# A two-layer graph convolution on one core: batches of twelve tiles instead of eight, rings of two batches, and TensorE's wait for target one-hots placed behind the next gathers

## The reference, cut to what matters

```python
# emb 18750 x 64, W1 64 x 128, W2 128 x 64, edge_index 2 x 300000, r_input 512 x 200
def gcn_conv(x, W, b, src, dst, n):
    h = x @ W
    deg = jnp.zeros((n,), h.dtype).at[dst].add(1.0) + 1.0
    dinv = jax.lax.rsqrt(deg)
    norm = dinv[src] * dinv[dst]
    agg = jax.ops.segment_sum(h[src] * norm[:, None], dst, num_segments=n)
    return agg + h * (dinv * dinv)[:, None] + b
h = gcn_conv(emb, W1, b1, src, dst, 18750)
nodes = gcn_conv(h, W2, b2, src, dst, 18750)
return nodes[r_input.reshape(-1)].reshape(512, 200, 64)
```

## Time and profile before

| what | value |
|---|---|
| median of 3 runs | 2710.62 us (2710.17 to 2713.58) |
| the profiled execution's own time | 2695.12 us |
| its span, first to last instruction | 2693.2 us |
| mean granted TensorE clock in it | 0.867 |
| TensorE matmul busy | 2067.8 us (77%) |
| VectorE busy | 2301.0 us (85%) |
| ScalarE busy | 1928.6 us (72%) |
| GpSimd busy | 927.8 us (34%) |

### The profile page before, as it was taken

One profiled execution on the slowest core, in us unless ns is written; L12 is line 12 of the kernel. 1 busy time (PEld: TensorE's weight loads), 2 busy tenths in 40 slices (PEclk: granted clock), 3 DMA queues, 4 the chain that ended last, 5 costly groups with the idle time before them and its releaser, 6 DMA issues.

```text
span 2693.2 us, 87729 instructions
## 1 busy us (share of the span) xinstructions
PE 2067.8 (77%) x36895; PEld 1728.1 (64%) x36895; DVE 2301.0 (85%) x3709; ACT 1928.6 (72%) x5267; POOL 927.8 (34%) x704
## 2 busy tenths in 40 slices
PE   3455555554562699998889899989999999999980
PEld 2345454444321477787777777867888888888870
DVE  9999999999988689889889999967777777777760
ACT  7868999999663886666666667766777777777760
POOL 2000000000000345426735456314233446666666
PEclk8566666665786899999999999999999999999995
DMA  4000000000021334343347555566776764555531
GB/s 115 0 1 1 1 1 1 1 1 1 18 71 43 107 117 133 118 136 105 98 113 139 123 133 148 147 186 186 211 214 212 210 193 142 139 143 139 145 106 18
DMA packets 191626, 277.10 MB, mean 103 GB/s; under 512 B 122459, under 2 KB 130539, under 8 KB 190973
## 3 DMA queue, kind: packets, MB, share of 16 engines
q1 hardware_dynamic: 168924, 244.05, 28.8%
q0 software_dynamic: 22304, 27.40, 8.3%
HBM read 219.68 MB, written 51.81 MB: 101 GB/s over the span
## 4 chain that ended last, share of the span: by engine, by line
PE 49%; DVE 36%; ACT 6%; issue 4%; POOL 2%; DMA 2%; SPq 0%; DVEq 0%; POOLq 0%
PE ps L1366 27%; PE ps L1315 16%; DVE keys L1610 7%; DVE keys L1611 7%; DVE oh L1946 4%; DVE oh L1460 4%; DVE arena L1460 3%; ACT arena L1118 1%; ACT grow_t L1044 1%; DVE keys L1872 1%; PE ps L1251 1%; DVE keys L1630 1%; DVE keys L1631 1%; PE ps L1341 1%; POOL out L912 1%
## 5 line engine op out<-in xcount | busy, mean ns | idle before, releaser
L1133 ACT ACTIVATE grow_t<-ps 128x384 bf16<-128x384 f32 x2744 | 1144.1, 498 | 525.1 <-PE ps L1315 489.3
L1366 PE MATMUL ps<-grow_t,oh 128*128 128x192 bf16 x10952 | 1054.0, 248 | 4.1 <-issue 3.5
L1366 PEld LDWEIGHTS ps<-grow_t,oh 128*128 128x128 bf16 x10952 | 880.5, 98 | 124.2 <-issue 105.6
L1946 DVE TENSOR_TENSOR oh<-iorep,dl 128x2048 bf16<-128x2048 bf16 x686 | 833.1, 1218 | 118.2 <-PE ps L1366 96.9
L1315 PE MATMUL ps<-arena,keys 128*32 128x192 bf16 x21952 | 608.0, 249 | 63.8 <-DVE keys L1872 23.9
L951 POOL DMA_INDIRECT zring<-table,sidx x296 | 397.2, 1342 | 513.4 <-PE ps L1315 462.7
L1315 PEld LDWEIGHTS ps<-arena,keys 128*32 128x32 bf16 x21952 | 429.2, 97 | 195.1 <-issue 130.4
L859 POOL DMA_INDIRECT arena<-line,row_i x22 | 30.1, 1368 | 832.8 <-DVEq L1688 825.9
L1044 ACT ACTIVATE grow_t<-colf,arena 128x128 bf16<-128x128 f32 x992 | 294.3, 394 | 7.6 <-PE ps L1179 7.6
L1872 DVE TENSOR_SCALAR keys<-keys,rowf 128x2048 bf16<-128x2048 int16 x344 | 260.1, 756 | 30.8 <-DMA keys<-srel 20.8
L1610 DVE TENSOR_TENSOR keys<-keys 128x1280 f32<-128x1280 f32 (+4 forms) x212 | 246.3, 1162 | 13.1 <-ACT keys L1097 9.9
(11 more groups left out here) (246 smaller groups left out, 1912.5 us busy)
## 6 DMA issues: line engine op xcount, KB each, us to landing
keys<-srel SPq DMA_DIRECT2D x344, 512.0 KB
out<-res SPq DMA_DIRECT2D x50, 512.0 KB
table<-arena SPq DMA_DIRECT2D x19, 384.0 KB, 2.8
table<-sgn_l SPq DMA_DIRECT2D x73, 96.0 KB
arena<-table SPq DMA_DIRECT2D x5, 960.0 KB, 8.7
zring<-table,sidx POOLq DMA_INDIRECT x296
nodes<-arena SPq DMA_DIRECT2D x73, 64.0 KB
arena<-in_L_rec_edge_index SPq DMA_DIRECT2D x2, 1171.5 KB, 5.3
```

The lines of the kernel that those rows point to most:

```text
L1133: act.activation(grow[:, (layer * NB + j) % DEEP, h * 2 * ROW:(h + 1) * 2 * ROW], psum[HALF_BANK[layer][HB * j + h][0]][:, 0:2 * ROW], ACT ...
L1366: mm = pe.matmul(sums(sl, k), dwin[:, (layer * NB + j) % DEEP, t // TT, k * P:(k + 1) * P, t % TT], grow[:, (layer * NB + j) % DEEP, t * R ...
L1946: dve.tensor_tensor(dwin[:, (layer * NB + j) % DEEP, 0:made[1], :, :], iorep[:, :, :].unsqueeze(1).to_broadcast(made), dl_h[:, j * BT:j * ...
```

## The change

`BT` goes from 8 to 12, so that a layer has 229 batches of 6 halves (2748 tiles gathered, 10 of them empty, against 2744). `DEEP` goes from 3 to 2: both rings hold 24 tiles as before. Source one-hots are built 12 tiles at a time instead of 16, one build a batch and two batches ahead; their input ring has three places instead of two (`RBUFS`). `AHEAD` is 6 halves, again one batch. TensorE's wait for `d_ready` and `surplus(j)` move behind the gathers of batch j+1. The batch numbers of everything else are scaled by about two thirds: a preparation every 3.5 batches instead of 5, with `TO_QUARTER`, `TO_REL`, `TO_DST` of 3, 6, 8 instead of 4, 9, 12; `LATE_STEP` 2 instead of 3; a guest holds its bank for 3 batches instead of 4. By these numbers there are 42 minis instead of 40.

```diff
-BT = 8
+BT = 12
-DEEP = 3
+DEEP = 2
-RBUFS = 2
-PT = 2 * BT
-NP = -(-NB // 2)
-AHEAD = 4
-LEAD = 7
+RBUFS = 3
+PT = BT
+NP = NB
+AHEAD = HB
+LEAD = 5
...
-        RANKED = 2 * (GT - EARLY) + 1
+        RANKED = -(-2 * 2 * (GT - EARLY) // 3) + 1
...
-            return 5 * (g - 1)
-
-        TO_QUARTER, TO_REL, TO_DST = 4, 9, 12
+            return 7 * (g - 1) // 2
+
+        TO_QUARTER, TO_REL, TO_DST = 3, 6, 8
...
-        ROUNDS, LIST_STEP, LATE_STEP = OU // 8, 5, 3
-        ROUND_AT = LIST_AT + 9
+        ROUNDS, LIST_STEP, LATE_STEP = OU // 8, 3, 2
+        ROUND_AT = LIST_AT + 6
...
-        STORED_AT = [UNITS[1][upto - 1][2] + 10 for upto in UPTO]
-        FILL_FROM, FILL_STEP, FILLS = 20, 3, RT // FILL
+        STORED_AT = [UNITS[1][upto - 1][2] + 8 for upto in UPTO]
+        FILL_FROM, FILL_STEP, FILLS = 17, 2, RT // FILL
...
-                    guest_at[guest] = take(j, guest, j + 4)
+                    guest_at[guest] = take(j, guest, j + 3)
...
-                    wait_ge(rel_out, 16 * (p * PT // P + 1))
+                    wait_ge(rel_out, 16 * (min(p * PT + PT - 1, DO - 1) // P + 1))
...
-                    if x and x % (2 * HB) == 0:
-                        pe.wait_ge(s_ready, layer * NP + FREE + x // (2 * HB) + 1)
+                    if x and x % HB == 0:
+                        pe.wait_ge(s_ready, layer * NP + FREE + x // HB + 1)
...
-                    pe.wait_ge(d_ready, layer * NB + j + 1)
                     if layer == 0:
...
-                    surplus(j)
                     for x in range(HB * j + AHEAD, HB * j + AHEAD + HB):
                         if x < HB * NB:
                             gather_half(x)
 
+                    pe.wait_ge(d_ready, layer * NB + j + 1)
+                    surplus(j)
                     for h in range(HB):
...
                 s_build(0)
+                s_build(1)
...
-                    if j % 2 == 0 and j // 2 + 1 < NP:
-                        s_build(j // 2 + 1)
+                    if j + 2 < NP:
+                        s_build(j + 2)
```

More of the change, by code:

```diff
@@ L513, in gcn_program @@
         LIST_AT = PREPARED + 3
[L514 to L515 removed]
+        ROUNDS, LIST_STEP, LATE_STEP = OU // 8, 3, 2
+        ROUND_AT = LIST_AT + 6
         MASK_AT = ROUND_AT + LIST_STEP * (ROUNDS - 1) + 10
         OVER_AT = MASK_AT + 1
[L518 to L519 removed]
+        LISTED = OVER_AT + 10
+        EARLY_ROUNDS, ROUND_STEP = 6, 4
         PICK_AT = LIST_AT + 5
@@ L522, in gcn_program @@
         DEALS = list(range(0, DONE8, WRAP))
-        ORDER_AT = DEAL_AT + 20
+        ORDER_AT = DEAL_AT + 14
         BAD_AT = ORDER_AT + 2 * (QG + 2)
@@ L526, in gcn_program @@
         LATE = [sl for sl in range(SPE) if close_batch(sl) - 2 < LISTED]
-        FETCHES = [(max(prep_at(g) - 4, 0), "rank", g, 0) for g in range(2, GT)]
+        FETCHES = [(max(prep_at(g) - 3, 0), "rank", g, 0) for g in range(2, GT)]
         FETCHES += [(max(prep_at(g) - 1, 0), "cell", g, 0) for g in range(1, GT)]
-        FETCHES += [(prep_at(g) + 2, "quarter", g, q) for g in range(1, GT) for q in range(1, WIN)]
+        FETCHES += [(prep_at(g) + 1, "quarter", g, q) for g in range(1, GT) for q in range(1, WIN)]
         FETCHES += [(ROUND_AT + LIST_STEP * (u // 8) - 1, "unit", u, 0) for u in range(OU)]
@@ L568, in gcn_program @@
         NU = len(UNITS[0])
-        LAG = 9
+        LAG = 7
         assert all(b[2] - a[2] > LAG + 1 or b[2] == NB for a, b in zip(UNITS[0], UNITS[0][UR:]))
@@ L615, in issued @@
                     if t + 1 in BOUNDS:
-                        scatters += [(max(HB * SCATTER_AT, at + 10 * HB), n) for n in COLS_OF[SET_OF[t]]]
+                        scatters += [(max(HB * SCATTER_AT, at + 7 * HB), n) for n in COLS_OF[SET_OF[t]]]
                 elif scatters and at >= scatters[0][0]:
@@ L798, in _ @@
                     if layer == 0:
-                        for name, g in prep_steps(p - 6):
+                        for name, g in prep_steps(p - 4):
                             if name == "rel":
                                 rel_store(g)
-                        if p == LIST_AT + 1:
+                        if p == LIST_AT + 2:
                             list_rows()
-                        if p == LIST_AT + 5:
+                        if p == LIST_AT + 4:
                             list_load()
-                        if p == DEAL_AT + 7:
+                        if p == DEAL_AT + 6:
                             deal_store()
-                        if p - DEAL_AT - 10 in range(0, 3 * len(DEALS), 3):
-                            deal_load(DEALS[(p - DEAL_AT - 10) // 3])
-                    for unit in units_at(layer, p - 7 - lag):
+                        if p - DEAL_AT - 8 in range(0, 2 * len(DEALS), 2):
+                            deal_load(DEALS[(p - DEAL_AT - 8) // 2])
+                    for unit in units_at(layer, p - 5 - lag):
                         unit_out(layer, *unit)
-                    if p % 2 == 0 and (layer == 0 or p // 2 >= RBUFS):
-                        sources_in(layer, p // 2)
+                    if layer == 0 or p >= RBUFS:
+                        sources_in(layer, p)
                     if layer and p >= FILL_FROM and (p - FILL_FROM) % FILL_STEP == 0 and (p - FILL_FROM) // FILL_STEP <= FILLS:
                         fill_part((p - FILL_FROM) // FILL_STEP)
-                for j in range(NB - 7, NB + lag + 1):
+                for j in range(NB - 5, NB + lag + 1):
                     if layer == 0:
@@ L1141, in _ @@
                     if layer == 0 and 1 <= j < RANKED:
-                        rank(EARLY + (j - 1) // 2, (j - 1) % 2)
+                        for n in range((j - 1) * 3 // 2, min(j * 3 // 2, 2 * (GT - EARLY))):
+                            rank(EARLY + n // 2, n % 2)
                     if layer == 0:
@@ L1828, in prepare @@
                     rows_by_act(EARLY, GT, 2 * (GT - 1))
-                if j == LIST_AT - 5:
+                if j == LIST_AT - 3:
                     dve.sem_inc(over_ready, 1)
@@ L1863, in prepare @@
                     dve.sem_inc(flag_ready, 1)
-            assert PICK_AT > LIST_AT + 2 and FLAG_AT + 20 < NB
+            assert PICK_AT > LIST_AT + 2 and FLAG_AT + 14 < NB
             dve.wait_ge(w_made, 3)
@@ L1870, in s_build @@
                     if p >= SBUFS:
-                        dve.wait_ge(gmm, HB * layer * NB + 2 * HB * (p - SBUFS + 1))
+                        dve.wait_ge(gmm, HB * layer * NB + HB * (p - SBUFS + 1))
                     dve.tensor_scalar(s_oh[:, p % SBUFS, :], srow[:, p % RBUFS, :], rowf[:, 0:1], None, ALU.is_equal).then_inc(s_ready, 1)
```

4 lines of the change are left out of this document (2 added, 2 removed).

## The result

The changed kernel takes 2751.5 us in the median (2749.7 to 2758.9, 4 runs) beside 2712.0 us for the kernel before on the same chip (2710.2 to 2713.6, 4 runs): a ratio of 1.0156 with an interval of 1.0137 to 1.0176. The forecast was 2679 us, its range ended at 2717, and the sign is wrong. Executions that took far longer than the others of their kernel (3202 us in r3, 4224 us in e14) are left out of medians and ratios. Later runs fell on other chips, and there the picture splits. On two more chips the change gave 1.0175 (1.0158 to 1.0192) and 1.0167 (1.0134 to 1.0199); on a fourth it gave 1.0001 (0.9990 to 1.0011), 2679.5 against 2680.5 us. I call the first three chips the first kind (the kernel before takes 2696 to 2712 us there) and the others the second (2680 to 2683 us).

A forecast was written before the change was run, and what follows sets the result against it. TensorE was taken to bound layer 1 and VectorE most of layer 0. Layer 1 -36, layer 0 0 and the end +4.5 summed to -32 us: 2679 us from a median of 2710.6, range 2652 to 2717.

The forecast's parts named there:

- the price of a batch: Layer 1, TensorE: two mode switches of 0.16 us cost 0.32 per batch; 114 fewer batches save 36.5 us.
- the ring of two at nothing: Target one-hot builds: slack shrinks from 2.05 to 1.3 us but stays positive, so two batches of room cost nothing.
- 2655: Rival, layer 0 gains too: the moved wait removes VectorE's 22 us of waits for TensorE; chance 0.16.
- 2715: Rival: the drain is no switch price and grows with the group, so nothing is saved; chance 0.06.
- With no guest in layer 1 ... nothing: Layer 1 PSUM banks: half x takes the bank of half x-6, copied a batch ago, at no cost.
- Bank waits "most hidden": Layer 0: guests' banks make gathers wait 55 us, mostly hidden behind VectorE, busy 99% in 1440 to 1740; +8 us taken.
- banks eat it: Rival, 2708 us: over half of the 55 us of bank waits lie bare, +30 in layer 0; chance 0.12.
- My slack of 1.3 us: Layer 1: a target build has 4.2 us available; the worst batch has 2.9 us in front of d_ready.
- The rival's mechanism: Rival, ring of two, 2742 us: VectorE over 3.3 us a batch makes layer 1 scatters wait for one-hots; chance 0.14.
- The list wait: Layer 0: the 11.6 us wait for GpSimd's surplus list shrinks by 5, to 5 to 7 us.
- the durations of both builds: VectorE: a target build of 3072 columns takes 1.75 us, a source build of 1536 takes 0.62.
- the end: GpSimd alone behind the last gathers: 22 instead of 18 early DMAs are left over, 54 in all, +4.5 us.

The follow-up runs named there:

- r3: The changed kernel with the d_ready wait and surplus products ahead of the next gathers again, first kind of chip: 2770.0 us, 1.0233 of the kernel before.
- e14: Batches of ten tiles with rings of three, guests keeping their bank for 4 batches, second kind: 2664.0 us, 0.9930 of the kernel before.
- e2: The kernel before (eight tiles, rings of three) with only the wait and surplus products moved behind the next gathers, second kind: 2681.5 us, 0.9999.
- e4: The kernel before with GpSimd's 92 early output lookups and stores moved behind the last batch, second kind: layer 1 at 792.8 us.
- e3: The changed kernel with GpSimd's 92 early output lookups and stores moved behind the last batch, second kind: layer 1 at 770.4 us.
- e15: The changed kernel with the 92 lookups and stores behind the last batch, run again, second kind: layer 1 at 781.8 us.
- e16: The changed kernel with the 92 lookups and stores behind the last batch, run once more, second kind: layer 1 at 774.8 us.
- e10: The changed kernel with GpSimd's layer 1 indirect transfers set to start when a gather run has ended, first kind: 2768.4 us, 1.0230 of the kernel before.
- e11: The changed kernel with GpSimd's layer 1 indirect transfers set to start 0.2 us into a gather run, first kind: 2770.3 us, 1.0228 of the kernel before.
- r1: The changed kernel run again unchanged on another chip of the first kind: 2743.4 us, 1.0175 of the kernel before.
- r2: The changed kernel run again unchanged on a further chip of the first kind: 1.0167 of the kernel before.
- r4: The changed kernel run unchanged on a chip of the second kind: 2679.5 us, 1.0001 of the kernel before.
- e8: The changed kernel with three batches of room for target one-hots and guests keeping banks for 4 batches, first kind: 2728.4 us, 1.0124 of the kernel before.
- e5: The changed kernel with batches of ten tiles (runs of 40 gathers), rings of two, first kind: 2712.4 us, 1.0060 of the kernel before.
- e1: The changed kernel with the d_ready wait and surplus products ahead of the next gathers again, second kind: 2689.6 us, 1.0034 of the kernel before.
- e6: The changed kernel with each batch's 48 gathers split into two runs of 24, first kind: 2746.7 us, 1.0193 of the kernel before.

## Why the prediction failed

The forecast was -36 us in layer 1 and 0 in layer 0. Measured were +15.1 and +39.1, on the kind of chip of the first comparison. In layer 1 two steps of the sum failed: the price of a batch, and the gathers' runs, which got no term although they grew by half. In layer 0 the ring of two at nothing failed, and the runs again. The range was also wider than its text said: three rivals lay in it (2655, 2708, 2715), not two.

**The price of a batch (0.32 us): mis-sized.** A batch of twelve without surplus takes 3.19 us, not 3.15. Then 2.20 x 1.5 - 3.19 = 0.11 us go per new batch, so the fixed price is 0.22 and 114 batches save 25 us a layer, not 36.5. I had added the two idle times of 0.16 to the groups' busy spans, but those spans grow by more than half: in a batch without surplus 24 scatters take 1.93 us where 1.5 x 1.27 is 1.91, 48 gathers 0.95 where I had 0.92. The better source was the pace inside a run: 1.27 us for 16 loads contains a first step of 0.015, 14 steps of 0.083 and one load's own length of 0.10. On the second kind layer 1 does give 20.4 us (797.5 in e2 to 777.1), near the 25; with the lookups behind it the gain is 11 to 22 us (e4 against e3, e15, e16).

**No term for longer runs: they break.** "With no guest in layer 1 ... nothing" holds for the banks. But on the first kind of chip, runs of 48 gathers are interrupted 99 times in layer 1 for 40.5 us (4.1 before). These 36 us more are over the 25 us saved and make 11 of the 15.1 us by which layer 1 ends longer. The interruptions are shown, and so are their growth with the length of the run and their going with the kind of chip. That GpSimd's transfers cause them is argued only: on the first kind 0.60 to 0.99 of the runs under such transfers break in e10, e11, r1, r2 and r3 as in the changed kernel, but on the second kind the same overlap does nothing, and the runs that were to take transfers away fell on that kind. A second sign fits: TensorE's sequencer records its wait behind the gathers 0.535 us after a whole run's first gather (median of 136 runs), when 28 of 48 gathers have started, so it is 40 instructions ahead; in interrupted runs the record lies at 1.15 us (90 runs). On the second kind it lies at 0.54 us under undisturbed transfers too (105 runs of r4). So on the first kind something holds the sequencer up by 0.6 us, which a run of 32 may be too short to feel; that is an argument and no run shows it. The Trainium skill gives 64 as TensorE's queue depth in Advanced Engine Details and Errata, Engine Queue Depths; the 40 is below it, and no run here shows a full queue. The loading of instructions, a rival, is not what goes with the breaks: of the runs of layer 1 under an undisturbed transfer 0.87 of 47 break with a load of the instruction queue (16 KB, 134 in the layer) within 0.3 us of them, and 0.84 of 50 without. What differs between the chips stays open; each chip ran in one group of runs only, so a chip and its occasion are not told apart either.

**Bank waits "most hidden": size right, cover open on the first kind.** 55 us were forecast and 55.8 measured. On the second kind layer 0 has 48 us more inside its runs, less 25 at switches, and grew by 4.2; I had 55 - 36 = 19 us more of TensorE's work and a layer unchanged. There the cover held. On the first kind 76 us more lie inside the runs, 61 of them at the start of a half, where the bank waits are, and 16 elsewhere, and the layer grew by 39.1. My reason for the cover was too wide: VectorE filled 99% of one stretch, and half of the waits lie ahead of it. On the first kind VectorE's waits for L1367 ahead of the build are 25.0 us where the kernel before had 16.1; on the second they are 12.4. But two runs speak against the banks as the main loss. e8 has 32 us more of these waits than r1 and a shorter layer 0, and e5, whose runs have no more pauses inside than the kernel before, still takes 18 us more. The rival "banks eat it" is thus not borne out. How the 39 us divide among the ring, the broken runs and the banks no run tells; that 35 of them are missing on the second kind, which has hardly any breaks, is the strongest sign for the breaks.

**The ring of two at nothing:** 15 us or more by e8, 13 of them in layer 0. My slack of 1.3 us was worked out for layer 1, where the wait of L1948's readers is indeed 0.8 us. In layer 0, where VectorE's preparations and requests stand ahead of a build, I never made that sum. e5's layer 0 points the same way. The rival's mechanism (VectorE over 3.3 us a batch in layer 1) did not happen; the Trainium skill's rule in Perfetto Trace Analysis, Optimizing Scalar/DVE Operations, pointed at a part of the loss, but its case, larger builds as such, is not told apart from the smaller ring by any run.

**The list wait:** forecast 5 to 7 us, measured 14.3, against 11.6 before; in e1, e5 and r3 it was 6.1 to 7.7. Counting tiles between the slots did not give it. The moved wait is not the whole reason, since e5 and e6 have it too and wait 7.7 and 7.8 us; why it is longer in the changed kernel is open. The wait ahead of L1398 is 13.3 us on TensorE, 12.1 before.

**Right:** the durations of both builds, the wait's move out of TensorE's way in layer 1, the end (+4.5 forecast, +4.7 measured, with these 54 transfers; the earlier trace rows had 50):

```profile
L912 POOL DMA_INDIRECT out<-arena,oidx x31 | 30.6, 989 | 9.4 <-issue 9.4
L903 POOL DMA_INDIRECT arena<-nodes,oidx x16 | 15.2, 950 | 4.9 <-issue 4.9
L898 POOL DMA_INDIRECT arena<-nodes,oidx x7 | 6.7, 952 | 3.5 <-PE ps L1316 1.7 <-issue 1.5 <-DMA nodes<-arena 0.3
```

Put again with measured terms, second kind: -20 in layer 1, +4 in layer 0, +8 at the end (56 transfers there), -8 by the profiles, -1 in the medians. That layer 0 came within 4 us of the forecast there is partly luck, since the sum had nothing for the ring.

## What to carry to other kernels

A fixed price per batch is read from two batch sizes or from the step inside a run, not by adding the idle times between groups to their busy spans. Whether a wait is covered by another engine has to be worked out stretch by stretch and layer by layer: here VectorE was full in one stretch, and a slack worked out for layer 1 was taken for layer 0 as well. And before an experiment is compared with the run that it is to explain, both must have run on one chip: here the chip was worth more (30 us) than most edits.

## What was not expected of the hardware

- Two kinds of chip for one program: the kernel before takes 2680 to 2683 us in four sets of runs on three chips, 2696 to 2712 on three others. Its layer 0 has 41.6 us inside the runs on the first kind and 21.9 on the second (e4).
- Narrow gathers, 20.6 ns apart, break after 13 to 47 of a run of 48, by 0.2 to 2.2 us, mostly where the program has no wait (96 of 99 places in layer 1).
- A GpSimd transfer that starts outside VectorE's builds takes 0.94 to 1.02 us, even where a build starts during it (115 in layer 1 of the changed kernel); one that starts inside a build takes 0.94 to 2.8, 1.9 in the median (190). The Trainium skill's page SBUF — State Buffer, SBUF: two separate sides, says that GpSimd can't write descriptors while VectorE runs an operation that holds the port pair that they share; the trace agrees. On the first kind of chip it is the undisturbed transfer, not the stretched one, that goes with the breaks in TensorE's stream (0.86 against 0.08).
